# Attention and MLP kernel on one core: where the input and the probabilities are transposed

## The chip, the cores and the metric

The kernel runs on one core of one Trainium2 chip. Its time is the device time of one execution, in microseconds. The kernel before took 1684.08 us, the median of 3 runs (1683.23 to 1684.34).

## The reference

The input x has 4 batches of 2048 rows of 512 float32 numbers. The first half is a causal attention with one head of 512:

```
x_norm = (x - mean) / sqrt(var + eps) * gamma + beta
q, k, v = x_norm @ wq, x_norm @ wk, x_norm @ wv
probs = softmax(causal(q @ k.T / sqrt(512)))
x1 = layernorm(x + (probs @ v @ wo + x))
```

The second half is an MLP of three 512x512 products with SiLU behind the first two, a softmax router over 8 experts of which the two best give gates, a scatter-add of gated rows into the first 8 rows, and a last layernorm.

## The kernel before

**Numbers.** Each large product is done as three fp32r products of split operands (`split_product`, L334 to L336): hi x hi, lo x hi and hi x lo. So each operand needs its hi part, which ScalarE or VectorE rounds, and its lo part, which VectorE gets as the difference (f32 value less hi).

**Opening.** The weights are folded into m = wq wk' and wvo = wv wo (`fold_weights`, TensorE), so that scores are (x_norm m) x_norm' and v is x_norm wvo.

**Stages.** A batch has 16 tiles of 128 query rows, in 4 groups of 4. Tile t has `chunks(t)` = t//4 + 1 chunks of keys, up to 512 keys each. Every engine has its own queue in a written order, in functions named `tile(b, t)`; the engines meet at semaphores. The loop over batches starts at tile 2 and has tiles 0 and 1 of the next batch at its end, so its back edge lies between tiles 1 and 2. On TensorE tile t is:

- scores of tile t+1, chunk after chunk, into one PSUM bank per chunk (12 matmuls for 512 keys), with the transposes of tile t's chunk 0 ahead of the last chunk;
- for each chunk of tile t: transposes of the next chunk's probabilities (`turn_probs`, L1221), then `attend`, the chunk's product with v (3 matmuls per 128 keys);
- in tiles 2, 6 and 10 the projections of the next group: `project_v` of its first tile, `project_g`, three more `project_v`. For the next batch's first group they lie in tile 15.

**Probabilities.** ScalarE's `exp` writes a row tile `probs` in SBUF. TensorE turns it in 128x128 blocks into one of two PSUM banks, ScalarE rounds it to `pt_hi` (L628), VectorE takes the difference to `pt_lo` (L859). Both have two buffers, so chunk n waits for `attend` of chunk n-2 (`pv_done`).

**Input.** x is loaded in pairs of tiles into `xin`, normalised in place (statistics on VectorE, L823; the reciprocal root on GpSimd; scale and shift on ScalarE, L580), turned by TensorE into PSUM (`turn_x`, L1159), given gamma and beta by ScalarE (L564), and split by VectorE (`split_x`, L841 and L843) into `xt_hi` and `xt_lo`. This is done in units of half a pair in the tiles ahead of the projections.

**VectorE's order in tile t** is: residual of tile t-1, maxima of tile t+1's chunks but the last, difference of chunk 0, last maximum and bias (`row_bias`), row sum, difference of chunk 1, the pieces for x, `norm_behind` (statistics of the outputs), and then the differences of chunks 2 and 3.

**SyncE's queue** issues, in order, each tile's load of x for the residual, and the stores of x1 and of the output of earlier tiles. In the last tile it also loads x1 for the second half, with `load_x1` (L345): rows of 32 elements, 128 bytes, laid out so that VectorE's transpose of 32x32 blocks (L994) gives the full transpose.

## Time and profile before

| | us |
|---|---|
| median of 3 runs | 1684.08 |
| profiled execution | 1682.32 |
| its span, first to last instruction | 1680.3 |
| TensorE busy | 1650.4 |
| VectorE busy | 828.1 |
| ScalarE busy | 671.6 |
| GpSimd busy | 282.6 |

Busy time of TensorE counts overlapping matmuls once. A row of the timeline gives the start, the duration, the engine and the line; x4 at its end means four in a row that were merged, and a bracket gives the idle time ahead and what ended it. The second number of a group is the mean duration of one. DMA moved 92.58 MB, at 55 GB/s over the span.

### The profile page before, as it was taken

What the parts mean: (1) busy time and instruction counts of PE and PEld (TensorE: products, weight loads), DVE (VectorE), ACT (ScalarE), POOL (GpSimd) and SP (SyncE); (2) the same over time, 40 slices, a digit from 0 to 9 for tenths busy, and PEclk for the clock granted to TensorE, in tenths of its full rate; (3) what the DMA queues carried; (4) which work ended last, traced back from release to release, by engine and by line L of the source; (5) the groups of instructions that cost most, each with busy time, mean ns of one, the idle gap of its engine ahead of it and who ended that gap; (6) DMA issues with size and microseconds to landing.
All of it is one profiled execution on the core that took longest, in us unless ns stands there. A gap on an engine that the chain in (4) does not pass through costs nothing.

```text
span 1680.3 us, 23574 instructions
## 1 busy us (share of the span) xinstructions
PE 1650.4 (98%) x7923; PEld 1369.7 (82%) x7923; DVE 828.1 (49%) x2168; ACT 671.6 (40%) x1301; POOL 282.6 (17%) x491
## 2 busy tenths in 40 slices
PE   7999999999999999999999999999999999999998
PEld 5888888878888888788888888888878888888886
DVE  5454434454453445455343456443456556555563
ACT  5443333443342334343322445332344444444443
POOL 1120201111120111121110112010122212212121
PEclk9999999999999999999999999999999999999999
DMA  4111201121111011121101132111154223132200
GB/s 157 57 51 51 70 32 38 64 71 63 70 51 51 32 50 64 58 101 49 53 19 38 45 100 95 38 57 45 63 115 74 36 39 50 25 50 43 32 0 7
DMA packets 173764, 92.58 MB, mean 55 GB/s; under 512 B 137296, under 2 KB 137296, under 8 KB 173664
## 3 DMA queue, kind: packets, MB, share of 16 engines
q1 hardware_dynamic: 162768, 72.41, 15.8%
q10 hardware_dynamic: 10896, 18.90, 3.6%
q8 instruction: 56, 0.92, 0.2%
q14 instruction: 44, 0.36, 0.1%
HBM read 57.71 MB, written 33.57 MB: 54 GB/s over the span
## 4 chain that ended last, share of the span: by engine, by line
PE 79%; issue 13%; POOL 3%; ACT 3%; DVE 2%; DMA 1%; SPq 0%; ACTq 0%; POOLq 0%; DVEq 0%
PE psum L334 24%; PE psum L336 24%; PE psum L335 24%; PE psum L1221 3%; PE psum L1159 1%; POOL rstd L454 1%; PE psum L1326 1%; PE psum L1325 1%; PE psum L1318 1%; PE psum L1317 1%; ACT xin L580 1%; ACT tok L580 1%; POOL expo L529 1%; ACT affine L564 0%; DVE stats L823 0%
## 5 line engine op out<-in xcount | busy, mean ns | idle before, releaser
L334 PE MATMUL psum<-xt_hi,g_hi 128*128 128x512 f32 (+3 forms) x640 | 239.5, 374 | 0.4 <-DVE g_lo L849 0.4
L628 ACT ACTIVATE pt_hi<-psum 128x512 fp32r<-128x512 f32 (+3 forms) x160 | 84.8, 530 | 369.6 <-PE psum L1221 363.7
L336 PE MATMUL psum<-xt_lo,g_hi 128*128 128x512 f32 (+3 forms) x640 | 230.0, 359 | 0.0
L335 PE MATMUL psum<-xt_hi,g_lo 128*128 128x512 f32 (+3 forms) x640 | 229.2, 358 | 0.0
L334 PE MATMUL psum<-v_hi,pt_hi 128*128 128x512 f32 x544 | 222.8, 410 | 1.8 <-DVE pt_lo L859 1.4
L336 PE MATMUL psum<-v_lo,pt_hi 128*128 128x512 f32 x544 | 213.1, 392 | 0.0
L335 PE MATMUL psum<-v_hi,pt_lo 128*128 128x512 f32 x544 | 212.8, 391 | 0.0
L451 POOL TENSOR_TENSOR var_eps<-meanvar,eps 128x2 f32<-128x2 f32 (+1 forms) x97 | 19.3, 199 | 1048.8 <-DVE meanvar L827 1046.7
L864 DVE TENSOR_REDUCE rowmax<-psum 128x1 f32<-128x512 f32 (+3 forms) x160 | 97.5, 610 | 197.7 <-PE psum L336 197.2
L746 ACT ACTIVATE act_f<-psum 128x512 f32<-128x512 f32 x128 | 76.5, 598 | 210.0 <-PE psum L336 210.0
L529 POOL TENSOR_TENSOR expo<-euler,shifted 128x32 f32<-128x32 f32 x16 | 86.9, 5430 | 298.0 <-DVE shifted L1061 298.0
L334 PEld LDWEIGHTS psum<-xt_hi,g_hi 128*128 128x128 f32 x640 | 121.2, 189 | 15.5 <-DVE g_lo L849 0.5
L859 DVE TENSOR_TENSOR pt_lo<-psum,pt_hi 128x512 fp32r<-128x512 f32 (+3 forms) x160 | 97.4, 609 | 73.4 <-ACT pt_hi L628 71.7
L336 PEld LDWEIGHTS psum<-xt_lo,g_hi 128*128 128x128 f32 x640 | 120.3, 188 | 16.1
L335 PEld LDWEIGHTS psum<-xt_hi,g_lo 128*128 128x128 f32 x640 | 120.8, 189 | 15.1
L336 PEld LDWEIGHTS psum<-v_lo,pt_hi 128*128 128x128 f32 x544 | 102.2, 188 | 22.9
L334 PEld LDWEIGHTS psum<-v_hi,pt_hi 128*128 128x128 f32 x544 | 102.3, 188 | 22.2 <-issue 2.9
L335 PEld LDWEIGHTS psum<-v_hi,pt_lo 128*128 128x128 f32 x544 | 102.6, 189 | 17.7
L580 ACT ACTIVATE tok<-tok,shift,rstd 128x512 f32<-128x512 f32 x128 | 97.3, 809 | 46.5 <-POOL shift L456 46.4
L849 DVE TENSOR_TENSOR g_lo<-psum,g_hi 128x512 fp32r<-128x512 f32 x64 | 44.2, 691 | 130.9 <-ACT g_hi L577 130.9
L612 ACT ACTIVATE probs<-psum,bias 128x512 f32<-128x512 f32 (+3 forms) x157 | 97.6, 628 | 25.1 <-PE psum L1221 11.9
L853 DVE TENSOR_TENSOR v_lo<-psum,v_hi 128x512 fp32r<-128x512 f32 x64 | 44.0, 688 | 121.4 <-ACT v_hi L602 121.4
(145 smaller groups left out, 3401.7 us busy)
## 6 DMA issues: line engine op xcount, KB each, us to landing
xin<-in_x ACTq DMA_DIRECT2D x64, 256.0 KB, 2.8
tok<-in_x SPq DMA_DIRECT2D x64, 256.0 KB, 2.6
x_scratch<-tok SPq DMA_DIRECT2D x64, 256.0 KB, 2.0
out_dram<-tok SPq DMA_DIRECT2D x64, 256.0 KB, 2.0
x_in<-x_scratch SPq DMA_DIRECT2D x64, 256.0 KB, 4.2
xin<-in_w_t ACTq DMA_DIRECT2D x8, 256.0 KB, 2.8
w_sb<-in_w_t SPq DMA_DIRECT2D x1, 1024.0 KB, 5.2
raw<-in_wq_t SPq DMA_DIRECT2D x1, 768.0 KB, 6.1
```

The source lines that it names most:

```text
L334: pe.matmul(o, ws, ms, start=first, stop=False, skip_group_check=True)
L335: pe.matmul(o, w_lo, ms, start=False, stop=False, skip_group_check=True)
L336: return pe.matmul(o, ws, m_lo_, start=False, stop=last, skip_group_check=True)
L529: pool.tensor_tensor(expo[:], euler[:], shifted[:], ALU.pow).then_inc(exp_ready, 1)
L580: return act.activation(o, y, ACT.Identity, bias=shift[:, slot:slot + 1], scale=rstd[:, slot:slot + 1])
L612: act.activation(probs[:, at:at + w], psum[:, c, 0:w], ACT.Exp, bias=bias[:, t % 2:t % 2 + 1], scale=SCALE, accum_out=sums4[:, t % 2, c:c ...
L628: act.activation(pt_hi[:, n % 2, 0:w], psum[:, turn_bank(turn_use(t, c)), 0:w], ACT.Copy).then_inc(pt_hi_ready, 1)
L746: act.activation(act_f[:, n % 2, :], psum[:, bank, :], ACT.Silu)
L849: dve.tensor_tensor(g_lo[:, j, :], psum[:, j, :], g_hi[:, j, :], ALU.subtract).then_inc(g_ready, 1)
L859: dve.tensor_tensor(pt_lo[:, n % 2, 0:w], psum[:, turn_bank(turn_use(t, c)), 0:w], pt_hi[:, n % 2, 0:w], ALU.subtract).then_inc(pt_ready, 1)
L864: return dve.tensor_reduce((rowmax if chunks(t) == 1 else rowmax4)[:, c:c + 1], psum[:, c, 0:width(t, c)], AX.X, ALU.max)
L1221: last = pe.transpose(psum[:, turn_bank(n), k * P:(k + 1) * P], probs[:, key_start(t, c) + k * P:key_start(t, c) + (k + 1) * P], ident[:])
```

## The change

Three things are changed.

- The normalised pairs of x are stored to DRAM (`xn_scratch`), loaded back as 128-byte rows into `xt_b` (the memory of `xt_lo`) and turned by VectorE into `xt_a` (the memory of `xt_hi`), a group of four tiles at a time; ScalarE applies gamma and beta back into `xt_b`, and VectorE splits from there, in four units of 128 x 512. The first group of the first batch is still turned by TensorE.
- The probabilities of tiles 8 to 15 (`FAR`) take the same way: SyncE stores each chunk to `p_scratch`, loads it back into `probs` as 128-byte rows, and VectorE turns it into `pt_f` (the memory of `pt_lo`).
- In the opening TensorE does 14 matmuls of the identity, the fold is ordered anew, and three pairs of x are loaded early into a free part of `xt_a`.

The diff, cut to its core:

```diff
+    FAR = 2 * GROUP
+    P_BLOCK = P * GROUP * P
+    p_scratch = nc.dram_tensor("p_scratch", [2 * GROUP * P_BLOCK], F32, kind="Internal").ap()
     x1_scratch = nc.dram_tensor("x1_scratch", [B * S, D], F32, kind="Internal").ap()
+    xn_scratch = nc.dram_tensor("xn_scratch", [B * S, D], F32, kind="Internal").ap()
...
+        unrounded = ExitStack()
+        xt_a = sb("xt_a", [P, DC, S], F32, unrounded)
+        xt_b = sb("xt_b", [P, DC, S], F32, unrounded)
+        unrounded.close()
         xt_hi = sb("xt_hi", [P, DC, S], F32R, stage01)
         xt_lo = sb("xt_lo", [P, DC, S], F32R, stage01)
-        affine = sb("affine", [P, 512], F32, stage01)
...
+        turned = ExitStack()
+        pt_f = sb("pt_f", [P, 2, GROUP * P], F32, turned)
+        turned.close()
         pt_lo = sb("pt_lo", [P, 2, GROUP * P], F32R, stage01)
...
+        def x_pair(n, first):
+
+            if first and n in EARLY:
+                return xt_a[:, n - 1, 2 * GROUP * P:4 * GROUP * P].rearrange("p (s d) -> p s d", s=2)
+            return xin[:]
...
+        def columns(g):
+            return slice(GROUP * g * P, GROUP * (g + 1) * P)
+
+        def through_dram(b, t, c):
+
+            tiles_with = [u for u in range(FAR, TILES) if chunks(u) > c]
+            return b * len(tiles_with) + tiles_with.index(t) + 1
+
+        def p_rows(t, c):
+
+            at = (t % 2 * GROUP + c) * P_BLOCK
+            return p_scratch[at:at + P * width(t, c)]
...
+                if pair == 1:
+                    for n in EARLY:
+                        sp.dma_start(x_pair(n, True), pair_rows(x, 0, n)).then_inc(x_early_loaded[n - EARLY[0]], DMA)
...
+            def store_p(b, t, c):
+                w, at = width(t, c), key_start(t, c)
+                sp.wait_ge(probs_ready, 1 + b * CHUNKS + BEFORE[t] + c + 1)
+                sp.dma_start(p_rows(t, c).rearrange("(r n) -> r n", n=w), probs[:, at:at + w]).then_inc(p_stored[c], DMA)
+
+            def load_p(b, t, c):
+
+                w, at = width(t, c), key_start(t, c)
+                sp.wait_ge(p_stored[c], through_dram(b, t, c) * DMA)
+                rows_of = p_rows(t, c).rearrange("(r j k q i) -> q j k r i", j=LANES, k=w // P, q=QUADRANTS, i=LANES)
+                for q in range(QUADRANTS):
+                    sp.dma_start(probs[q * LANES:(q + 1) * LANES, at:at + w].rearrange("j (k r i) -> j k r i", k=w // P, i=LANES),
+                                 rows_of[q]).then_inc(p_loaded[c], DMA)
...
+            def store_xn(b, pair, first=False):
+                sp.wait_ge(x_normed, b * PAIRS + pair + 1)
+                sp.dma_start(pair_rows(xn_scratch, b, pair), x_pair(pair, first)).then_inc(xn_stored, DMA)
+
+            def load_x(b, pair):
+                sp.dma_start(xin[:], pair_rows(x, b, pair)).then_inc(x_loaded, DMA)
+
+            def load_xq(b, g):
+
+                rows_of = xn_scratch[bass.ds(b * S + g * (GROUP * P), GROUP * P), :].rearrange("(t j) (c q i) -> q j c t i", j=LANES, q=QUADRANTS, i=LANES)
+                for c in range(DC):
+                    for q in range(QUADRANTS):
+                        sp.dma_start(xt_b[q * LANES:(q + 1) * LANES, c, columns(g)].rearrange("j (t i) -> j t i", i=LANES),
+                                     rows_of[q][:, c]).then_inc(xq_loaded[g % 2], DMA)
...
+                g, k = t // GROUP, t % GROUP
                 slot = t % SLOTS
                 sp.wait_ge(out_stored[slot], 1 + (b * USES + t // SLOTS) * DMA)
                 sp.dma_start(tok[:, slot, :], x[bass.ds(b * S + t * P, P), :]).then_inc(res_loaded[slot], DMA)
+                if t == TILES - 1 and not last:
+                    sp.wait_ge(scores_ready, b * CHUNKS + BEFORE[t] + 1)
+                    load_xq(b + 1, 0)
+                normed = None
...
+                if normed:
+                    store_xn(*normed)
+                if t >= FAR:
+                    for c in range(chunks(t)):
+                        store_p(b, t, c)
+                    for c in range(2):
+                        load_p(b, t, c)
...
+                if t >= FAR:
+                    for c in range(2, chunks(t)):
+                        load_p(b, t, c)
+                if normed:
+                    sp.wait_ge(xn_stored, stored(*normed))
+                    to_load = ahead(b, first_half(g) if k else second_half(g), last)
+                    if to_load:
+                        load_x(*to_load)
+                if k == GROUP - 1:
+                    if g + 2 < GROUPS:
+                        sp.wait_ge(scores_ready, b * CHUNKS + 1)
+                        load_xq(b, g + 2)
+                    elif g + 2 > GROUPS and not last:
+                        sp.wait_ge(scores_ready, b * CHUNKS + BEFORE[t] + 2)
+                        load_xq(b + 1, g + 2 - GROUPS)
...
+            for t in range(2):
                 tile(0, t, before=False)
+            for n in EARLY[0:2]:
+                store_xn(0, n, first=True)
+            sp.wait_ge(xn_stored, stored(0, EARLY[1]))
+            load_xq(0, 1)
+            store_xn(0, EARLY[2], first=True)
+            tile(0, 2, before=False)
...
+            def affine_x(b, g, c):
+
+                act.wait_ge(xq_turned, (b * GROUPS + g - 1) * DC + c + 1)
+                act.activation(xt_b[:, c, columns(g)], xt_a[:, c, columns(g)],
+                               ACT.Identity, bias=beta_sb[:, c:c + 1], scale=gamma_sb[:, c:c + 1]).then_inc(affine_ready, 1)
...
+                if t == 1 and not before:
+                    norm_x(b, EARLY[2], first=True)
+                if k == 2 and ahead(b, second_half(g), last):
+                    norm_x(*ahead(b, second_half(g), last))
                 if more and k == 2:
-                    turn_x(b, g + 1, 2)
-                if t == TILES - 2 and not last:
-                    turn_x(b + 1, 0, 0)
+                    affine_x(b, g + 1, 2)
+                    affine_x(b, g + 1, 3)
                 if t == TILES - 1 and not last:
-                    turn_x(b + 1, 0, 2)
-                if more and k == 1:
-                    norm_x(b, 2 * (g + 1) + 1)
+                    affine_x(b + 1, 0, 2)
+                    affine_x(b + 1, 0, 3)
...
+                if k == GROUP - 1 and ahead(b, first_half(g), last):
+                    norm_x(*ahead(b, first_half(g), last))
                 if t and not (t == TILES - 1 and not last):
                     norm_behind(b, t - 1, (0, 1) if before or t > 1 else (0,))
+                if more and k == 1:
+                    affine_x(b, g + 1, 0)
+                    affine_x(b, g + 1, 1)
                 if t == TILES - 2 and not last:
-                    norm_x(b + 1, 1)
+                    affine_x(b + 1, 0, 0)
+                    affine_x(b + 1, 0, 1)
...
+                    else:
+                        act.wait_ge(xn_stored, stored(B - 1, PAIRS - 1))
...
+            def norm_x(b, pair, first=False):
+                if first and pair in EARLY:
+                    dve.wait_ge(x_early_loaded[pair - EARLY[0]], DMA)
+                else:
+                    dve.wait_ge(x_loaded, (pair + 1) * DMA if first else (b * PAIRS + pair - 2) * DMA)
+                if not first or pair:
+                    dve.wait_ge(x_normed, b * PAIRS + pair)
+                y = x_pair(pair, first)
+                statistics(lambda s: y[:, s - 2, :], 2, 4, x_variance)
+
+            def split_first_x(u):
+                at = slice(2 * (u // 2) * P, 2 * (u // 2 + 1) * P)
+                c = slice(2 * (u % 2), 2 * (u % 2) + 2)
+                dve.wait_ge(affine_ready, 1 + u + 1)
+                dve.tensor_copy(xt_hi[:, c, at], xt_b[:, c, at]).then_inc(xt_hi_ready, 1)
+                dve.wait_ge(xt_hi_ready, u + 1)
+                dve.tensor_tensor(xt_lo[:, c, at], xt_b[:, c, at], xt_hi[:, c, at], ALU.subtract).then_inc(xt_ready, 1)
+
+            def turn_x(b, g, c):
+                dve.wait_ge(xq_loaded[g % 2], (2 * b + (g + 1) // 2) * DC * LOADS)
+                dve.transpose(xt_a[:, c, columns(g)], xt_b[:, c, columns(g)]).then_inc(xq_turned, 1)
+
+            def split_x(b, g, c):
+                n = (b * GROUPS + g) * XUNITS + c + 1
                 dve.wait_ge(affine_ready, 1 + n)
-                dve.tensor_copy(xt_hi[:, c:c + 2, at:at + 256], value).then_inc(xt_hi_ready, 1)
+                dve.tensor_copy(xt_hi[:, c, columns(g)], xt_b[:, c, columns(g)]).then_inc(xt_hi_ready, 1)
                 dve.wait_ge(xt_hi_ready, n)
-                dve.tensor_tensor(xt_lo[:, c:c + 2, at:at + 256], value, xt_hi[:, c:c + 2, at:at + 256],
+                dve.tensor_tensor(xt_lo[:, c, columns(g)], xt_b[:, c, columns(g)], xt_hi[:, c, columns(g)],
                                   ALU.subtract).then_inc(xt_ready, 1)
...
+            def turn_probs(b, t, c):
+
+                n, w, at = BEFORE[t] + c, width(t, c), key_start(t, c)
+                dve.wait_ge(p_loaded[c], through_dram(b, t, c) * LOADS)
+                dve.wait_ge(pv_done, 1 + b * CHUNKS + n - 1)
+                dve.transpose(pt_f[:, n % 2, 0:w], probs[:, at:at + w]).then_inc(probs_turned, 1)
 
             def chunk_max(b, t, c):
                 dve.wait_ge(scores_ready, b * CHUNKS + BEFORE[t] + c + 1)
@@ -903,37 +1047,37 @@
                 more = g + 1 < GROUPS
                 if t:
                     residual(b, t - 1)
-                if t + 1 < TILES:
-                    for c in range(chunks(t + 1) - 1):
-                        chunk_max(b, t + 1, c)
+                early_maxima = range(chunks(t + 1) - 1) if t + 1 < TILES else range(0)
+                for c in early_maxima[0:1]:
+                    chunk_max(b, t + 1, c)
+                if t >= FAR:
+                    turn_probs(b, t, 0)
+                for c in early_maxima[1:]:
+                    chunk_max(b, t + 1, c)
                 split_probs(b, t, 0)
-                if more and k == 0:
-                    split_x(b, g + 1, 0)
+                if t >= FAR:
+                    turn_probs(b, t, 1)
                 if t + 1 < TILES:
                     row_bias(b, t + 1)
                 row_sum(b, t)
                 if chunks(t) > 1:
                     split_probs(b, t, 1)
-                if more and k == 0:
+                if more and k == 1:
+                    for c in range(DC):
+                        turn_x(b, g + 1, c)
+                if more and k == 2:
+                    split_x(b, g + 1, 0)
                     split_x(b, g + 1, 1)
-                if more and k == 2:
-                    split_x(b, g + 1, 2)
-                if t == TILES - 2 and not last:
-                    split_x(b + 1, 0, 0)
                 if t == TILES - 1 and not last:
                     split_x(b + 1, 0, 2)
-                if k == 3 and g + 2 < GROUPS:
-                    norm_x(b, 2 * (g + 2))
-                if k == 3 and g + 2 == GROUPS and not last:
-                    norm_x(b + 1, 0)
+                if k == GROUP - 1 and ahead(b, first_half(g), last):
+                    norm_x(*ahead(b, first_half(g), last))
                 if t:
                     norm_behind(b, t - 1, z=2 if before or t > 1 else 1)
                 elif before:
                     norm_behind(b - 1, TILES - 1)
                 if t + 1 < GROUP:
...
                 if t == TILES - 1 and not last:
                     split_x(b + 1, 0, 3)
...
                 if chunks(t) > 2:
+                    if t >= FAR:
+                        turn_probs(b, t, 2)
                     split_probs(b, t, 2)
...
                 if chunks(t) > 3:
+                    if t >= FAR:
+                        turn_probs(b, t, 3)
                     split_probs(b, t, 3)
                 if t == TILES - 1 and last:
                     split_wr()
+                if t == TILES - 2 and not last:
+                    for c in range(DC):
+                        turn_x(b + 1, 0, c)
+                    split_x(b + 1, 0, 0)
+                    split_x(b + 1, 0, 1)
                 if more and k == 2:
+                    split_x(b, g + 1, 2)
                     split_x(b, g + 1, 3)
                     split_v(b, GROUP * (g + 1))
...
+                if t == 0 and not before:
+                    norm_x(b, EARLY[2], first=True)
+                if k == 1 and ahead(b, second_half(g), last):
+                    norm_x(*ahead(b, second_half(g), last))
...
-                    pe.wait_ge(xt_ready, 1 + b * (GROUPS * XUNITS) + g * XUNITS + 3 + half)
+                    pe.wait_ge(xt_ready, 1 + b * (GROUPS * XUNITS) + g * XUNITS + (3 + half if first else 2 + 2 * half))
...
+                if tile % GROUP == 0 and tile:
+                    pe.wait_ge(xt_ready, 1 + (b * GROUPS + tile // GROUP + 1) * XUNITS)
...
             def turn_probs(b, t, c):
+                if t >= FAR:
+                    return
...
                 turn_probs(b, t, 0)
-                if more and k == 0:
-                    turn_x(b, g + 1, 0)
                 if t + 1 < TILES:
                     score(b, t + 1, chunks(t + 1) - 1)
...
+            for _ in range(WARMING):
+                pe.matmul(psum[:, XBANK, 0:P], ident[:], ident[:], start=True, stop=True)
+            fold_weights(0, 0, (0, 1))
+            turn_x(0)
+            fold_weights(0, 0, (2, 3))
+            turn_x(1)
+            for c in range(1, DC):
+                fold_weights(0, c, range(DC))
+            for c in range(2):
+                fold_weights(1, c, range(DC - 1))
+            turn_x(2)
+            for c in range(2, DC):
+                fold_weights(1, c, range(DC - 1))
+            turn_x(3)
+            for c in range(DC):
+                fold_weights(1, c, (DC - 1,))
```

## Rows read from the trace of the kernel before

**Rows 1.** The page, part 1: busy time, share of the span, instructions.
```profile
PE 1650.4 (98%) x7923; PEld 1369.7 (82%) x7923; DVE 828.1 (49%) x2168; ACT 671.6 (40%) x1301; POOL 282.6 (17%) x491
```
**Rows 2.** What TensorE waited for: us in total, times, longest.
```profile
PE psum L1159 <- ACT xin L580: 11.9, 5, 9.4
PE psum L1221 <- issue: 4.7, 2, 2.4
PE psum L1159 <- ACT affine L564: 2.1, 4, 0.5
```
**Rows 3.** TensorE's groups by form, the transposes: busy us, mean ns, idle before.
```profile
L1221 PE MATMUL psum<-ident,probs 128*128 128x128 f32 x544 | 85.4, 272 | 4.8 <-issue 4.7
L1159 PE MATMUL psum<-ident,xin 128*128 128x128 f32 x256 | 39.6, 278 | 14.0 <-ACT xin L580 11.9 <-ACT affine L564 2.1
```
**Rows 4.** Timeline of TensorE in tile 12 of batch 1: start, duration.
```profile
573.92 0.60 PE L1221 MATMUL psum<-ident,probs 128*128 128x128 f32 x4
574.28 0.48 PE L334 MATMUL psum<-v_hi,pt_hi 128*128 128x512 f32 x1
574.60 0.39 PE L335 MATMUL psum<-v_hi,pt_lo 128*128 128x512 f32 x1
574.83 0.39 PE L336 MATMUL psum<-v_lo,pt_hi 128*128 128x512 f32 x1
```
**Rows 5.** Timeline of VectorE in the same tile.
```profile
574.12 0.42 DVE L864 TENSOR_REDUCE rowmax<-psum 128x1 f32<-128x256 f32 x1 [0.23 <-PE psum L336]
...
575.26 0.69 DVE L859 TENSOR_TENSOR pt_lo<-psum,pt_hi 128x512 fp32r<-128x512 f32 x1
575.87 1.28 DVE L823 BATCH_NORM_STATS2 stats<-tok 128x6 f32<-128x512 f32 x2
...
577.28 0.15 DVE L827 BATCH_NORM_AGGREGATE meanvar<-stats 128x2 f32<-128x6 f32 x1
```
**Rows 6.** VectorE's and ScalarE's groups by form.
```profile
L994 DVE STREAM_TRANSPOSE x1t_f<-x_in 128x512 f32<-128x512 f32 x64 | 41.6, 688 | 2.7 <-DMA x_in<-x_scratch 2.7
L859 DVE TENSOR_TENSOR pt_lo<-psum,pt_hi 128x256 fp32r<-128x256 f32 x28 | 11.9, 424 | 25.3 <-ACT pt_hi L628 25.0
...
L628 ACT ACTIVATE pt_hi<-psum 128x512 fp32r<-128x512 f32 x100 | 59.5, 596 | 324.1 <-PE psum L1221 321.1 <-issue 3.0
L628 ACT ACTIVATE pt_hi<-psum 128x256 fp32r<-128x256 f32 x28 | 10.6, 378 | 16.5 <-PE psum L1221 16.5
```
**Rows 7.** Timeline of VectorE in tile 2 of batch 1.
```profile
375.48 0.43 DVE L841 CAST xt_hi<-affine 128x512 fp32r<-128x512 f32 x1
375.94 0.69 DVE L843 TENSOR_TENSOR xt_lo<-affine,xt_hi 128x512 fp32r<-128x512 f32 x1
```
**Rows 8.** Timeline of TensorE in tile 2 of batch 1.
```profile
370.32 0.54 PE L1221 MATMUL psum<-ident,probs 128*128 128x128 f32 x3 [2.39 <-issue]
...
373.61 0.60 PE L1159 MATMUL psum<-ident,xin 128*128 128x128 f32 x4
...
379.36 0.39 PE L334 MATMUL psum<-wvo_hi,xt_hi 128*128 128x512 f32 x1
```
**Rows 9.** Timeline of TensorE from tile 14 to tile 15 of batch 0.
```profile
325.57 0.60 PE L1221 MATMUL psum<-ident,probs 128*128 128x128 f32 x4
...
327.76 0.47 PE L334 MATMUL psum<-v_hi,pt_hi 128*128 128x512 f32 x1
```
**Rows 10.** Timeline of TensorE in the opening.
```profile
10.10 0.78 PE L334 MATMUL psum<-raw_hi 128*128 128x512 f32 x1
10.68 0.63 PE L335 MATMUL psum<-raw_hi,raw_lo 128*128 128x512 f32 x1
...
37.89 0.39 PE L334 MATMUL psum<-xt_hi,m_hi 128*128 128x512 f32 x1
```
**Rows 11.** Timeline of SyncE's DMA queue in the last tile.
```profile
1232.20 11.44 SPq L345 DMA_DIRECT2D x_in<-x_scratch  x8
```
**Rows 12.** Timeline of VectorE in the last tile.
```profile
1240.79 1.31 DVE L994 STREAM_TRANSPOSE x1t_f<-x_in 128x512 f32<-128x512 f32 x2 [2.69 <-DMA x_in<-x_scratch]
```
**Rows 13.** Two windows: engines' busy time, granted clock, DMA share, GB/s.
```profile
1238.00:1240.00 2.00, 2.00 (x13) 1.65 (x12) 0.10 (x2) 0.60 (x1) 1.66 (x6) 1.00 1.00 158
10.00:15.00 5.00, 5.00 (x15) 3.98 (x14) 3.52 (x6) 2.58 (x5) 0.00 (x0) 1.00 1.06 403
```

More of the change, by code:

```diff
@@ L213, in attention_mlp @@
                 TURNS += [("v", t + 1 + j) for j in range(GROUP)]
-            TURNS += [("p", t, c) for c in range(chunks(t))]
+            if t < FAR:
+                TURNS += [("p", t, c) for c in range(chunks(t))]
         def turn_use(t, c):
@@ L497, in batch @@
                         tile(b + 1, t)
-            for pair in range(FIRST_PAIRS):
+            for pair in range(FIRST_PAIRS - 1):
                 norm_x(0, pair)
@@ L662, in tile @@
                         turn_probs(b, t, c)
-                    if more and k == 2 and c == chunks(t) - 1:
-                        turn_x(b, g + 1, 3, more=not (last and g + 2 == GROUPS))
                     if c < n_next:
@@ L934, in tile @@
                     split_v(b, t + 1)
-                if t == TILES - 2 and not last:
-                    split_x(b + 1, 0, 1)
                 if t == TILES - 1 and not last:
@@ L959, in tile @@
                         split_v(b, GROUP * (g + 1) + j)
-                if more and k == 0:
-                    norm_x(b, 2 * (g + 1) + 1)
-                if t == TILES - 2 and not last:
-                    norm_x(b + 1, 1)
+                if t == 0 and not before:
+                    norm_x(b, EARLY[2], first=True)
+                if k == 1 and ahead(b, second_half(g), last):
+                    norm_x(*ahead(b, second_half(g), last))
                 from_tile = TILES - 1 - GROUP
```

198 lines of the change are left out of this document (84 added, 114 removed).

## The prediction

> **What bounds the kernel now.** I read the page's busy shares first [rows 1]: TensorE is busy 98% of 1680.3 us, VectorE 49%, ScalarE 40%. So TensorE's queue is the kernel, and whatever leaves it is worth its issue time. Then what TensorE waited for [rows 2]: 11.9 us for the normalised input, of which 9.37 us is the opening, 4.7 us at the loop's back edges, 2.1 us for the affine step. There is next to no idle time to win; only instructions can be taken away, and every wait that is added counts in full. Third, the transposes by form [rows 3]: 544 of probabilities and 256 of x, with a duration of 272 to 278 ns.
>
> That duration is not the price, because matmuls overlap. The price is read from starts [rows 4]: four transposes start at 573.92, the next product at 574.28, so 0.36 us; and the first product behind them takes 0.32 us to the next start where its successors take 0.23. Together 0.45 us for four, 0.113 us each.
>
> **Removed from TensorE.** Probabilities of tiles 8 to 15: 9+10+...+16 = 100 blocks in each of 4 batches, 400. Of x: 256 less the 16 of the first group, 240. 640 x 0.113 = 72.5 us. With them go about 3 us of waits for x and affine behind the opening [rows 2]. ScalarE's copy and VectorE's difference stay, only from another source.
>
> The Trainium skill (TensorE: Matmul & The Clock Gate, Part 4: PE-mode transpose) gives about 275 ns for one transpose in a kernel, and the trace agrees as a duration. By it the 640 would be worth 176 us and the kernel would come to about 1506; the starts of rows 4 show the pace, so I don't use it.
>
> **Moved to VectorE.** 100 x 4 blocks of probabilities and 240 of x, in units like the 128x512 transpose that stage 2 has, 0.688 us, a new one about every 0.61 [rows 6]. It is half idle, so the sum of 100 us is no concern; its order is. The p transposes of chunks 0 and 1 stand ahead of the last score and are covered. That of chunk 2 can't be early: its buffer is shared with chunk 0, and VectorE reaches it only after the statistics. In the old order TensorE had turned the chunk already, so that behind the statistics only a difference was left.
>
> Let S be TensorE's start of the first thing behind the last score. In tile 12 [rows 4, 5] S is 573.92; the maximum starts at S+0.20, the difference of chunk 1 at S+1.34, the statistics at S+1.95, and they end at S+3.51 (577.28+0.15). A wider next chunk adds 0.1 to 0.2 us (0.42 us for 256 elements [rows 6], 0.69 for 512). From there the new chain of chunk 2 is transpose, round, difference: 0.69+0.60+0.69 and 0.2 for handovers, 2.2 us at 512 wide (1.4 at 256: 0.42+0.38+0.42 [rows 6]; 1.8 at 384). TensorE wants chunk 2 after two products of 12 matmuls, 2 x 2.72 = 5.44 behind S. One batch, tile by tile:
> - 8: about 0. 12: about 0. 13 and 14: S+5.7 and S+5.8, together 0.7 us.
> - 9: four transposes of x stand ahead of the statistics, +2.44: S+7.4, 2.0 us.
> - 10: two split units of x stand there, each 1.07 us (0.46 from 375.48 to 375.94, 0.61 for the difference) [rows 7], +2.14: S+7.6, 2.2 us. The second two end some 0.1 us late for the projection.
> - 11: the input's statistics stand there, 1.5 us, as before, but with the transpose behind them: S+7.1, 1.6 us (last batch 0.2).
> - 6: no chunk 2, but the projection of tile 8's v now waits for all four units of x: S + 2.0 + 4 x 1.07 + 1.5 = 7.8, with handover 8.0, wanted at 5.25: 2.8 us.
> - 2: the same, in a shorter tile. S was 373.61, the projection began at 379.36 with two transpose groups before it, so it is wanted at S+4.9 [rows 8]. VectorE had its maximum and sum at S+1.8 [rows 7], half a microsecond later now since tile 1 gained transposes; 2.3 + 4.28 + 1.5 + 0.6 + 0.2 = 8.9: 4.0 us.
> - 15: in tile 14 four transposes and two split units of the next batch stand behind the last difference. It ends near S+7.3; 2.4 for the transposes and 2.3 for the splits bring the residual to S+12.1; residual 0.7, transpose, round and difference 2.2: the first product at S+15.0, where tile 14's last one ended at S+10.7. 4.3 us; before, the gap was 2.19 [rows 9], of which 12 transposes were 1.36 and 0.83 idle. So 3.5 us, three times.
>
> Per batch 0.7+2.0+2.3+1.6+2.8+4.0 = 13.4 us; four batches less 1.4 for the last tile 11 are 52.2, tile 15 adds 10.5.
>
> **Last tile of all.** x1 for stage 2 is loaded by the same SP queue, now behind 1 MB of probability loads. Eight such 256 KB issues took 11.44 us [rows 11], so 1 MB holds SP for 5.7 us. The last exp is at about S+7.5; store, 5.7 us of loads, the other stores between them 1, then 5.7 us of x1 and its landing 2.9 (1240.79 less 1237.92 [rows 11, 12]): about S+24. VectorE waits for it in order, ahead of chunk 2's transpose; 1.3 for two transposes and 2.2 for the chain give S+28, where TensorE could have been there at S+20: 8 us. With 1.5 us at its first product that is 9.5.
>
> **DMA itself.** Otherwise the round trip is covered: exp of the last chunk is some 3 us before the tile's end, and VectorE asks for the first loaded chunk 3.5 us into the next tile, the second 3 us later. 26 MB of p and 16 MB of x come back in short rows. In stage 2 such a load kept the queues at a share of 1.00 at 158 GB/s [rows 13], so a 1 MB tile costs 7 us of a tile of some 22. The cost of the covered part is 0; if each came 2 us late in 32 tiles, +64; below 0 it can't be, for nothing in it replaces TensorE work. I take 0, its nearest rows being 7 of 22.
>
> Here the Trainium skill speaks against the change: DMA: Bandwidth & Descriptors (Specifications) wants at least 512 bytes a transfer for line rate, and these rows are 128 bytes. The trace agrees: 158 GB/s against 403 with the weights' long rows at 10 to 15 us [rows 13].
>
> **Opening.** TensorE starts at 9.37 on x, now on the weights at about 7.7, after 14 warming matmuls; its first products went at a pace of 0.43 (10.10 to 10.68 and on), half the later one, at a granted clock shown as 1.00 [rows 10, 13]. About 5 us of slow pace hold 2.3 us of loss. The fold's last quarter is put last, which covers x's second pair. The fold ended at 37.89 [rows 10]; 96 products need 21.8 us, the chain of weights lets the second half go from 22.3, and I get 32 to 34: -5 us (bounds 0 and -8). Two early pairs normalised on ScalarE, 3 us, lie beside the projection of g.
>
> **Sum.** 1682.3 (the profiled execution, 1.8 under the median of 1684.1): -72.5 -3 -5 +52.2 +10.5 +9.5 = 1674.0; on the median's footing 1675.8. I say 1676.
>
> **Rivals.**
> A. The DRAM trip is late (slower). Mechanism: SP's queue is in order; it stands at exp of the last chunk and only then sends loads of a tile, and VectorE's in-order queue stops at the first missing chunk with the maxima behind it. For: 1.43 us per 256 KB of issue. Against: some 2 us of slack at chunk 0 and 1.5 behind it. It decides once a load is over 3 us later than I have it; at 2 us in 24 four- or three-chunk tiles, +48: 1722.
> B. The waits are half hidden. VectorE's blocks would have to end sooner than their rows; against it is that each is a sum of measured durations. 72 halved: 1640.
> C. The clock falls in the new gaps (slower). The loop's gap of 2.39 us was followed by a first product at ordinary pace [rows 8], but seven new gaps are about 4 us and one is 8. If each is followed by the opening's slow stretch, 2.3 us: 8 x 2.3 = +18: 1694. The Trainium skill (TensorE: Matmul & The Clock Gate, Why this matters for your kernels) warns of idle gaps between bursts; no row here has one in mid-kernel longer than 2.39.
> D. The change moves the work without freeing time: waits of all kinds sum to the removed 72 to 80: within 3 us of 1684.
>
> **Chances.** Forecast 0.50, A 0.10, B 0.17, C 0.15, D 0.08. 0.2% is 3.4 us, about what a measurement of this kernel can tell from none. The forecast's own range is 1664 to 1690 (28 waits, each good to 0.4 us), of which seven in ten lie below 1680.7 and one in ten above 1687.5. Faster 0.35+0.17+0.02 = 0.54, same 0.16, slower 0.30. Range 1640 to 1704: B's centre, and a part of A.
>
> **What would show it.** L1221's transposes fall to 144 and x's to 16, and the sum of TensorE's work falls by 72 us. In a tile-10 stretch the first product of chunk 2 waits about 2 us for pt_lo. The projection behind tiles 2 and 6 waits 4 and 3 us for xt_lo. TensorE's idle time is about 30 - 8 + 72 = 94 us. In the last tile VectorE waits for x1 near 8 us. If VectorE waits for DMA in most tiles, A; if products pace at 0.43 behind the gaps, C. Wrong altogether if idle time is under 50 or over 130 us.

## The result and the profile after

The changed kernel takes 1771.18 us (median of 4 runs, 1763.91 to 1772.61) where the one before took 1683.78 beside it: 1.0506 times as long, 95% interval 1.0492 to 1.052. I had said 1676, with a range of 1640 to 1704. The sign was wrong.

The page, part 1, answers to [rows 1]; the span grew from 1680.3 to 1768.6 us:

```profile
PE 1629.9 (92%) x7311; PEld 1330.3 (75%) x7311; DVE 929.5 (53%) x2340; ACT 664.8 (38%) x1241; POOL 290.2 (16%) x491
```

7923 - 640 + 28 is 7311: the transposes are gone and 14 warming matmuls (two instructions each) have come. But TensorE's busy time fell by 20.5 us and not by 67, its idle time (span less busy) rose from 29.9 to 138.7, and the mean granted clock fell from 1.000 to 0.970. Two things are to be explained: 109 us more idle, and work that ran slower. What TensorE waited for (us in all, times, longest), which answers to [rows 2], the transposes that are left (busy, mean ns), to [rows 3], and what VectorE waited for in DMA:

```profile
PE psum L354 <- DVE pt_lo L996: 78.4, 35, 9.3
PE psum L354 <- DVE xt_lo L979: 40.0, 15, 6.1
PE psum L1379 <- issue: 5.4, 2, 3.0
...
L1379 PE MATMUL psum<-ident,probs 128*128 128x128 f32 x144 | 24.0, 276 | 5.4 <-issue 5.4
...
DVE pt_f L1004 <- DMA probs<-p_scratch: 46.2, 31, 5.2
DVE stats L945 <- DMA xin<-in_x: 28.0, 5, 8.3
DVE xt_a L972 <- DMA xt_b<-xn_scratch: 9.3, 3, 3.6
```

The first three rows say who hands over last, not who is late: VectorE is half idle, and stands 46 us itself for probabilities that come back from DRAM. So each wait has to be followed one step further. TensorE's timeline at the five kinds of long waits, the bracket giving the wait:

```profile
342.50 0.80 PE L354 MATMUL psum<-v_hi,pt_hi 128*128 128x512 f32 x1 [8.01 <-DVE pt_lo L996]
343.10 0.63 PE L355 MATMUL psum<-v_hi,pt_lo 128*128 128x512 f32 x1
343.52 0.63 PE L356 MATMUL psum<-v_lo,pt_hi 128*128 128x512 f32 x1
...
401.29 0.79 PE L354 MATMUL psum<-wvo_hi,xt_hi 128*128 128x512 f32 x1 [6.08 <-DVE xt_lo L979]
...
512.78 0.76 PE L354 MATMUL psum<-v_hi,pt_hi 128*128 128x512 f32 x1 [3.55 <-DVE pt_lo L996]
...
554.18 0.50 PE L354 MATMUL psum<-v_hi,pt_hi 128*128 128x512 f32 x1 [1.93 <-DVE pt_lo L996]
...
1328.77 0.80 PE L354 MATMUL psum<-v_hi,pt_hi 128*128 128x512 f32 x1 [9.28 <-DVE pt_lo L996]
```

They are tile 15 (batch 0), tile 2, tile 8, tile 10 and the last tile. For tile 8 my list had "about 0"; in batches 0 to 2 it is 3.9, 3.6 and 3.6 us. The chain of waits through it, in order of time (start, duration, what):

```profile
501.19 1.53 ACT xin L705 x2
...
502.74 0.42 SPq L457
...
503.27 2.84 DMA p_scratch<-probs
...
506.13 0.66 SPq L444
...
508.18 2.33 DMA probs<-p_scratch
...
510.53 0.72 DVE pt_f L1004
...
511.28 0.64 ACT pt_hi L755
...
511.94 0.70 DVE pt_lo L996
...
512.78 0.76 PE psum L354
```

and ScalarE's exp of the first chunk of that tile:

```profile
497.30 0.69 ACT L738 ACTIVATE probs<-psum,bias 128x512 f32<-128x512 f32 x1
```

The probabilities lay ready at 498.0. SyncE sent them only at 503.27, because its queue held the store of the normalised x first (L457), which waited for ScalarE until 502.7. From the store to the first loaded chunk it is 7.2 us (2.84, three issues before the fourth, 2.33 to land). Without the 5.3 us lost in the queue the chunk would have landed near 505.3, when VectorE came to ask for it (its last maximum ended at 505.69). The chunk had no slack to lose. The last batch has no next x to store, so there nothing stands ahead of tile 8's probabilities. The exp of its first chunk ended at 1153.36, and SyncE sent them at once:

```profile
1153.48 1.39 SPq L436 DMA_DIRECT2D p_scratch<-probs  x3
```

TensorE's first product of that tile waited for nothing (0.2 us between its start and the one before).

How SyncE's queue looks from tile 14 to tile 15:

```profile
323.34 8.73 SPq L467 DMA_DIRECT2D xt_b<-xn_scratch  x16
332.25 0.42 SPq L457 DMA_DIRECT2D xn_scratch<-xin  x1
332.78 2.35 SPq L436 DMA_DIRECT2D p_scratch<-probs  x4
335.92 5.39 SPq L444 DMA_DIRECT2D probs<-p_scratch  x8
```

Eight 64 KB loads hold it for 5.4 us, 0.67 us each, so a tile with four chunks costs it 10.7 us of load issues where I had 5.7. The size hardly counts here: four loads of 32 KB, in tile 8 of the last batch, took 2.55 us, 0.64 each. The sixteen loads of x come on top.

A third place is in tile 15, where SyncE gives out the next pair of x (L460) only at 348.16, behind all loads of probabilities. VectorE stood for it in batches 0 to 2 (6.1, 7.2 and 8.3 us, most of the 28.0 above), with the last split of x behind:

```profile
352.80 1.29 DVE L945 BATCH_NORM_STATS2 stats<-xin 128x6 f32<-128x512 f32 x2 [6.05 <-DMA xin<-in_x]
```

That split's end is what TensorE waited for inside `project_g` (0.9, 2.3 and 3.2 us).

The slower work is seen in windows of 1 us (us, busy time of each engine, then the granted clock, DMA share and GB/s), here around the wait at tile 15:

```profile
337.00:338.00 1.00, 0.00 (x0) 0.00 (x0) 0.97 (x3) 0.00 (x0) 0.00 (x0) 0.69 0.54 112
338.00:339.00 1.00, 0.00 (x0) 0.00 (x0) 1.00 (x2) 0.00 (x0) 0.00 (x0) 0.50 0.54 86
...
346.00:347.00 1.00, 1.00 (x4) 0.72 (x3) 0.71 (x2) 0.27 (x1) 0.00 (x0) 0.50 0.64 102
347.00:348.00 1.00, 1.00 (x5) 0.82 (x4) 0.00 (x0) 0.00 (x0) 0.00 (x0) 0.69 0.65 101
348.00:349.00 1.00, 1.00 (x6) 0.82 (x5) 0.00 (x0) 0.00 (x0) 0.00 (x0) 1.00 0.57 90
```

TensorE stopped at 334.5. The clock fell to 0.50, which is 1.2 instead of 2.4 GHz, 3 us later, and stayed there for about 5 us after work had begun again at 342.50; starts are 0.43 us apart in it (343.10, 343.52) and not 0.23. The same happens behind the waits of tile 2 in every batch, of tile 8 in the three that have one, and behind some of about 2 us.

### The profile page after: what moved, and what is told of

Its sections match the earlier page's. It is cut to its first block, busy times and chain, and to the rows that moved or that the text cites. A ratio compares the mean times of both kernels' runs of the same rounds, so it can differ in the third digit from the quotient of the medians.

```text
span 1768.6 us, 23775 instructions
## 1 busy us (share of the span) xinstructions
PE 1629.9 (92%) x7311; PEld 1330.3 (75%) x7311; DVE 929.5 (53%) x2340; ACT 664.8 (38%) x1241; POOL 290.2 (16%) x491
## 4 chain that ended last, share of the span: by engine, by line
PE 51%; issue 21%; SPq 9%; DVE 8%; DMA 5%; POOL 3%; ACT 3%; POOLq 0%; DVEq 0%; ACTq 0%
PE psum L354 16%; PE psum L356 16%; PE psum L355 16%; SPq L444 6%; DMA p_scratch<-probs 2%; DVE stats L945 2%; DMA xin<-in_x 1%; POOL rstd L583 1%; SPq L467 1%; DVE xt_a L972 1%; DMA probs<-p_scratch 1%; ACT xin L705 1%; PE psum L1475 1%; PE psum L1476 1%; PE psum L1468 1%
## 5 line engine op out<-in xcount | busy, mean ns | idle before, releaser
L354 PE MATMUL psum<-v_hi,pt_hi 128*128 128x512 f32 x544 | 226.2, 416 | 79.3 <-DVE pt_lo L996 78.4
L356 PE MATMUL psum<-v_lo,pt_hi 128*128 128x512 f32 x544 | 219.1, 403 | 0.0
L355 PE MATMUL psum<-v_hi,pt_lo 128*128 128x512 f32 x544 | 219.1, 403 | 0.0
L755 ACT ACTIVATE pt_hi<-pt_f 128x512 fp32r<-128x512 f32 (+2 forms) x112 | 65.7, 587 | 386.7 <-DVE pt_f L1004 377.4
L354 PEld LDWEIGHTS psum<-v_hi,pt_hi 128*128 128x128 f32 x544 | 106.3, 195 | 119.0 <-DVE pt_lo L996 71.9
L354 PE MATMUL psum<-wvo_hi,xt_hi 128*128 128x512 f32 x256 | 106.1, 414 | 33.6 <-DVE xt_lo L979 33.6
L356 PEld LDWEIGHTS psum<-v_lo,pt_hi 128*128 128x128 f32 x544 | 106.0, 195 | 23.9
L355 PEld LDWEIGHTS psum<-v_hi,pt_lo 128*128 128x128 f32 x544 | 106.4, 196 | 20.3
L354 PE MATMUL psum<-xt_hi,m_hi 128*128 128x512 f32 x256 | 101.2, 395 | 6.4 <-DVE xt_lo L979 6.4
```

The costliest lines, as they stand in the source:

```text
L354: pe.matmul(o, ws, ms, start=first, stop=False, skip_group_check=True)
L355: pe.matmul(o, w_lo, ms, start=False, stop=False, skip_group_check=True)
L356: return pe.matmul(o, ws, m_lo_, start=False, stop=last, skip_group_check=True)
L755: act.activation(pt_hi[:, n % 2, 0:w], turned_, ACT.Copy).then_inc(pt_hi_ready, 1)
```

## The experiments

Theory Q: SyncE's one in-order queue makes the two ways through DRAM disturb each other. Theory V: the order of VectorE's queue is the price, as the prediction had it. Theory C: the clock's fall is a large part. Each run's ratio is to the kernel before, measured beside it on the same chip, and runs are compared by these ratios; the changed kernel stands at 1.0506.

**The parts alone.** Three kernels; the first sets `FAR = TILES`, the second adds only `p_scratch`, `store_p`, `load_p` and VectorE's `turn_probs` to the kernel before, the third only the opening.

```diff
-    FAR = 2 * GROUP
+    FAR = TILES
```

> The changed kernel with the probabilities of all sixteen tiles turned by TensorE again; the input's way through DRAM and the opening stay. It saves 240 transposes (27 us) and 3 us of opening. If only VectorE's order costs (the waits of the prediction for tiles 2 and 6, 8 us a batch, less at tile 15), it gives 1684 - 27 - 3 + 36 = 1690. If the clock falls in each wait as well, some 16 us more: 1706. If the slow part is the way of the probabilities alone, it comes in at 1655.

> The kernel before with only the probabilities of tiles 8 to 15 sent through DRAM; input and opening as before. It saves 400 transposes (45 us). If the long waits at tiles 8 and 15 come from SyncE's queue, which then holds no store and no strided loads of x, they are gone, and only the last tile (13 us) and small waits (8 us) are left: about 1660, the best of these kernels. If instead the way of the probabilities is late in itself, tile 8 and tile 15 keep about 4 and 4 us a batch, with the clock's loss 45 us in all: about 1690.

> The kernel before with only the opening reordered: fourteen warming matmuls and the fold in the new order, nothing through DRAM. First group's projection starts 3 us earlier: 1680.5. If the early start is taken back by the first waits of batch 0: 1684.

Measured: input alone, with the opening, 1714.53 us (1.0176, 1.0159 to 1.0193); probabilities alone 1690.57 (1.0041, 1.0029 to 1.0054); opening alone 1679.43 (0.997, 0.9957 to 0.9982). So the opening gives 5 us (3 to 7), as forecast. Both ways through DRAM are a loss, each although it takes 27 or 45 us of work from TensorE. And alone they add 1.76% and 0.41%, together 5.06%: 2.9%, or 49 us (give or take 4), arises only when both are in. VectorE's order alone doesn't reach that: the waits in my list that need both parts, those of tiles 9, 10 and 15, come to 28 us at most. I was wrong, too, that the probabilities alone would give 1660.

**The clock.** Small matmuls nobody reads, ahead of the waits:

```diff
+            def fill(n):
+                for _ in range(n):
+                    pe.matmul(psum[:, XBANK, 0:P], ident[:], ident[:], start=True, stop=True)
...
                 n = BEFORE[t] + c
+                fill(FILL_A.get((t, c), 0))
```

> The changed kernel with small matmuls whose result nobody reads put into TensorE's queue just ahead of the waits: 32 ahead of the product for v of tile 4, 16 ahead of that of tile 8, 26 at tile 8, 12, 14 and 10 at tiles 9 to 11, 58 at tile 15, each 0.115 us and in sum shorter than the wait they stand in. They make nothing come sooner, so if waits alone cost the time stays at 1771 (no more than 5 us off). If the clock falls in the idle time and what follows then runs at half pace, idle time is as before counting the fillers but the granted clock goes from 0.97 to about 0.99 and the time falls by some 30 us, to about 1741.

Measured 1771.32 (1.0516, 1.0498 to 1.0534). The time did not move, but my price was wrong: each is two instructions and took 0.227 us, so the fillers were longer than the waits. It is still the most useful trace of the study, since the clock stays up until the last 12 us of it (0.999). Its page and the fillers' group:

```profile
PE 1737.5 (98%) x8655; PEld 1458.3 (82%) x8655; DVE 928.0 (52%) x2340; ACT 663.5 (37%) x1241; POOL 290.4 (16%) x491
...
L1339 PE MATMUL psum<-ident 128*128 128x128 f32 x1344 | 154.6, 275 | 0.0
```

1737.5 - 154.6 = 1582.9 us of real work at full clock. The kernel before had 1650.4; less 72.5 for the transposes and plus 5.3 for the warming makes 1583.2. So the forecast's 0.113 us a transpose was right, and the changed kernel's 1629.9 hold 47 us of slower work. Taken over the stretches at the lower clock, half of TensorE's busy time in them is 38 us; the other 9, as an estimate, are the ends and starts of matmuls at some 40 more stops. The Trainium skill (TensorE: Matmul & The Clock Gate, Part 4: PE-mode transpose) gives 275 ns; by that the work would have come down by 176 us, which this trace excludes.

Then half as many:

> As the kernel with the small matmuls, which took 0.227 us each and not 0.115, so that 58 of them lasted 13.1 us where the wait was 8.4. Here half as many: 16 before v of tile 4, 8 before v of tile 8, 13 at tile 8, 6, 7 and 5 at tiles 9 to 11, 29 at tile 15, 70 us in the whole run, all inside the waits. They make no data come sooner. Theory of the clock: the granted clock comes to 0.99 or more, the half-pace stretches behind the waits go, and the time falls by 35 to 45 us, to about 1730. Rival, that only the waits cost and the clock's fall lies inside them: 1771, no change.

Measured 1761.85 (1.0465, 1.0448 to 1.0483), clock 0.989:

```profile
PE 1683.6 (96%) x7983; PEld 1393.5 (79%) x7983; DVE 928.3 (53%) x2340; ACT 663.4 (38%) x1241; POOL 290.3 (17%) x491
...
L1339 PE MATMUL psum<-ident 128*128 128x128 f32 x672 | 79.8, 275 | 0.0
```

Real work is now 1683.6 - 79.8 = 1603.8, 26 us less than 1629.9. Fillers and idle together are 1759.6 - 1603.8 = 155.8 where 138.7 was idle: 17 us more. Of 26 us that the clock gave back, 9 (7 by the ratios, give or take 4) reached the end. That is somewhat too little, because at the end of the last batch fillers stood where the changed kernel hardly waits (tile 11) or waits less long (tile 15: 6.6 us of fillers, 3.8 of wait). At tile 10 of that batch, ahead of both, the kernel was 12.0 us ahead; of this one and of the changed kernel:

```profile
1192.45 0.50 PE L354 MATMUL psum<-v_hi,pt_hi 128*128 128x512 f32 x1 [0.36 <-DVE pt_lo L996]
...
1204.48 0.50 PE L354 MATMUL psum<-v_hi,pt_hi 128*128 128x512 f32 x1 [1.93 <-DVE pt_lo L996]
```

So about half of what the clock gave back can count. For the rest TensorE came sooner to its next wait and stood longer: before tile 8 of batches 0 to 2 it waited 2.8 to 2.9 us on top of 3.0 of fillers, where the wait was 3.6 to 3.9. Theory C holds for the mechanism and fails for the size: half or more of the slow pace is paid inside a chain that TensorE does not set.

**SyncE's queue.** First the store of x behind the probabilities at tiles 8 and 12, then the first group of x in 4 DMAs in place of 16 (the same bytes in long rows, so that those columns hold other values than the reference's). The edit of the first:

```diff
-                if normed:
+                late = t >= FAR and k == 0
+                if normed and not late:
                     store_xn(*normed)
...
+                if normed and late:
+                    store_xn(*normed)
```

> The changed kernel with one thing moved in SyncE's queue: at tiles 8 and 12 the store of the normalised x, which waits for ScalarE, comes behind the stores and the first loads of the probabilities. Theory of the queue: TensorE's wait at tile 8 (3.7 us, and about 1.8 us of slow work behind it) goes in all four batches, about 20 us: 1750. The rival, that the way through DRAM is late at tile 8 in itself: the wait shrinks by less than 1 us, 1768. The waits of tiles 2, 6, 9 to 11 and 15 stay in both.

> The changed kernel in which the first group of x of batches 1 to 3 is loaded by 4 DMAs instead of 16 (the same bytes in long pieces, so that those columns hold other values than the reference's). SyncE spends about 2.5 us instead of 8.7 there. Theory of the queue: VectorE's wait for that load (2.8 us) and the probabilities' delay (1.25 us) go, and TensorE's wait at tile 15 falls from 8.4 to 4.3 us, which VectorE's own work gives: about 13 us in three batches, 1758. If VectorE's work alone sets the wait: 1771.

Measured 1750.01 (1.0388, 1.0371 to 1.0406) and 1760.39 (1.0453, 1.0436 to 1.047). The first moves one line and gives 20 us (21 in microseconds), as expected, though from three batches and not four; TensorE's wait at tile 8 is gone. VectorE's wait for probabilities from DRAM, in that kernel:

```profile
DVE pt_f L1007 <- DMA probs<-p_scratch: 15.3, 16, 2.1
```

In the changed kernel it was 46.2 us in 31 waits. The second gives 9 (11 in microseconds): TensorE's wait at tile 15 falls from 8.01 to

```profile
341.10 0.80 PE L354 MATMUL psum<-v_hi,pt_hi 128*128 128x512 f32 x1 [5.84 <-DVE pt_lo L1002]
```

It changes two things at once, the number of DMAs and the length of their rows. And it does not free the whole 5.9 us that SyncE's issues of x became shorter, for the first store of probabilities, sent 4.2 us earlier, while the loads of x and the store behind them were under way, took 5.6 us to land and not 3.1. The chains of this kernel and of the changed one:

```profile
328.61 5.60 DMA p_scratch<-probs
...
332.78 3.13 DMA p_scratch<-probs
```

So near tile 15 what the transfers do to each other seems to count beside the queue; no run separates the two.

**VectorE's order.** The third chunk ahead of x and LayerNorm work, with and without a shift of x's split; and the latter's better form where only x goes through DRAM:

```diff
+                if t >= FAR:
+                    turn_probs(b, t, 2)
+                    split_probs(b, t, 2)
```

> The changed kernel with VectorE's and ScalarE's order changed: the third chunk of probabilities of tiles 8 to 15 is turned and split right behind the second and ahead of the work on x and the LayerNorm, and the split of the next x begins a tile earlier. If VectorE's order makes the waits, those at tiles 9, 10 and 11 (5.1 us a batch) go, that at tile 2 falls from 6.0 to about 1.2 us and that at tile 6 from 2.4 to 0; with the slow stretches behind them 12 to 17 us a batch: 1710 to 1725. If those waits are for DRAM and not for VectorE, they stay: 1765.

> The changed kernel with the order of the third chunk alone changed (the split of x stays where it was; in the run that moved both, VectorE then stood 3.8 us for ScalarE at the end of tiles 1, 5 and 9). VectorE's order: the waits at tiles 9, 10 and 11 go (5.1 us a batch, some 7 with the slow work behind them), 1771 - 25 = 1746. If TensorE then only waits at the next tile for what SyncE has not yet loaded, which that failed run would fit as well: 1765 to 1771.

> The kernel before with only the probabilities through DRAM, and the third chunk turned and split right behind the second, ahead of VectorE's work on x and the LayerNorm (in tiles 14 and 15 behind one part of x). In the kernel with the probabilities alone TensorE waited 1.6 to 1.9 us for that chunk at three tiles of every batch, and 1.9 to 2.1 more in tile 15. If VectorE's order makes these waits they go, 20 to 28 us with what is slow behind them: 1665. If the loads or ScalarE make them: 1690 as without the move.

> Only the input through DRAM (and the opening), with the four parts of x scaled a tile earlier and split together: TensorE's wait at tile 2 falls from 6.0 to about 2.7 us and that at tile 6 from 2.4 to 0, with what is slow behind them 25 us in all: 1714 - 25 = 1689. If, as with the third chunk, the wait only moves to TensorE's next stop: 1710.

Measured: 1772.55 (1.0531, 1.0513 to 1.0549); 1776.95 (1.056, 1.0543 to 1.0576); 1687.62 (1.002, 1.0011 to 1.003, where it was 1.0041 without the move); 1712.23 (1.0169, 1.0152 to 1.0186, where it was 1.0176). Four orders, and the most that any gained is 3.5 us. The waits that I named did go; others took their place. TensorE's waits with the third chunk first:

```profile
PE psum L354 <- DVE pt_lo L996: 70.7, 25, 10.9
PE psum L354 <- DVE xt_lo L979: 47.0, 14, 6.1
```

78.4 fell by 7.7 and 40.0 rose by 7.0: x was now late at tile 10 and the residual at tile 15. With only x through DRAM, the shifted split:

```profile
PE psum L354 <- DVE pt_lo L993: 31.5, 21, 3.3
PE psum L354 <- DVE xt_lo L976: 12.3, 5, 3.2
```

where the unshifted one had

```profile
PE psum L354 <- DVE xt_lo L979: 34.5, 12, 6.1
PE psum L354 <- DVE pt_lo L996: 13.6, 15, 1.9
```

The sum went from 48.1 to 43.8. Theory V as "a bad order" falls: the orders tried only chose which wait. VectorE is not full in these tiles either. In the run with the third chunk first it was busy 14.7 of the 19 us before tile 10's projection (212 to 231), and in the rest its queue stood in order for TensorE and ScalarE. In the run that shifted x as well, I had also made VectorE stand 3.8 us for ScalarE at the end of tiles 1, 5 and 9.

**The mends together.** All three orders, and the first load of x1 issued by ScalarE's queue, with VectorE's work on x1 behind its chunks of probabilities; the same for the probabilities alone; and the first with 4 DMAs for the first group of x.

```diff
+                    load_x1(act, 0, 0)
                     act.dma_start(wr_raw[:], wr_t.rearrange("(c p) n -> p c n", p=P)).then_inc(wr_loaded, DMA)
```

> The changed kernel with all the mends at once: the store of x behind the loads of the probabilities at tiles 8 and 12, the third chunk first, the four parts of x scaled at the end of the tile before and split together, and the first load of x1 given out by ScalarE's queue. If these orders are the whole price, 1771 - 21 - 25 - 10 - 10 = 1705, still above before, with the waits of tiles 2 and 15 left. If what is taken off one wait comes back in the next, since SyncE's queue in the last tiles and VectorE in tiles 1 and 2 are near full: 1735.

> The kernel before with the new opening, the probabilities alone through DRAM in VectorE's better order, and the first load of x1 given out by ScalarE's queue so that VectorE does not stand for it ahead of the third chunk. If the orders were all that spoiled this part: 1684 - 5 - 45 + 8 (small waits) + 10 (last tile, clock) = 1652 to 1665, faster than before. If DRAM's way is late in itself: 1680.

> All the mends together, and the first group of x of batches 1 to 3 loaded by 4 DMAs of long pieces instead of 16 (those columns then hold other values than the reference's). With all mends TensorE still waits 10 us at tile 15 of batches 0 to 2, while VectorE stands 3.8 us for this load. If SyncE's sixteen issues are the larger part: the wait falls to 5 or 6 us and the time by about 15 us, to 1702. If the probabilities' own way (store, wait, load, turn, round) sets that wait: below 2 us of gain, 1716.

Measured: 1717.6 (1.0197, 1.0181 to 1.0213); 1678.0 (0.9966, 0.9954 to 0.9978); 1708.95 (1.0142, 1.0118 to 1.0166). All mends take 52 us off the changed kernel. The parts alone, mended, stand at +1.69% (input with the opening) and -0.04% (probabilities, against the opening alone), together 1.65%, where both in one kernel stand at 1.97%. So of the 49 us that arose only from having both, some 5 are left, give or take 5. Which of the mends took how much of the rest, beyond the 20 of SyncE's order alone, was not tried one by one. At tile 15 the wait is 9.89 us with all mends, and with fewer issues

```profile
329.65 0.79 PE L354 MATMUL psum<-v_hi,pt_hi 128*128 128x512 f32 x1 [6.61 <-DVE pt_lo L1004]
```

so the loads of x, their number and short rows together, are a quarter to a third of that wait (10.08 to 7.79 and 9.70 to 6.26 in the next two batches); the 9 us gained lie between my two numbers.

The kernel with the probabilities alone, mended, is as fast as the one with the opening alone (0.9966 against 0.997). Both beat the kernel before by 5 to 6 us and the changed one by 90. TensorE's waits in it:

```profile
PE psum L345 <- DVE pt_lo L905: 26.2, 15, 8.9
PE psum L1224 <- ACT xin L622: 6.8, 3, 2.3
PE psum L1288 <- issue: 5.1, 2, 2.6
```

Its TensorE is busy 1621.6 us of a span of 1676.2, the opening alone has 1655.2 of 1678.9. It does 45 us less of transposes; busy time is 34 less (11 lost to half pace), idle time 31 more.

## Why the prediction was wrong

The terms of its sum, against the trace:

| step | said | measured |
|---|---|---|
| 640 transposes | -72.5 | -72.5 (1582.9 of work against 1583.2 worked out) |
| opening | -5 | -5.0 alone (3 to 7); the first projection at 34.54, not 32 to 34, against 37.89 [rows 10] |
| tile 2 | 4.0 a batch | 5.9, 6.1, 3.8, 6.0 |
| tile 6 | 2.8 | 2.4 to 2.5 |
| tiles 9, 10, 11 | 2.0, 2.3, 1.6 | 1.6 to 2.1, 1.9 and 0.5, 1.5 |
| tile 15 | 4.3 | 8.0 to 8.8, and 0.9 to 3.2 more inside `project_g` |
| last tile | 8 and 1.5 | 9.3 and 3.8 |
| tile 8 | 0 | 3.6 to 3.9 in batches 0 to 2, 0 in the last |
| TensorE idle | 94 | 138.7 |
| slower work | 0 | 47, of which 38 at the lower clock |

Work, slower work and idle time, 1583.2 + 47 + 138.7, make the span of 1768.6; the 47 is itself a difference, so what this confirms is the 1583.2 alone.

1. The step that failed first is "DMA itself": "The cost of the covered part is 0". It looked at bandwidth (7 us of 22) and not at the queue. At tile 8 the trip was just covered, with no slack for anything ahead of it in the queue. SyncE's in-order queue costs 20 us there (tile 12's line moved with it), shown by moving one line. The loads of x ahead of tile 15 cost 9 more, queue and transfer together. I had written the mechanism down as rival A, 0.10, but put it at the last exp and at "2 us of slack", and never walked SyncE's queue through a tile with `store_xn` and `load_xq` in it. Rival A's 1722 was the nearest of the rivals' numbers (it took 24 tiles of three or four chunks, where there are 32).
2. "Eight such 256 KB issues took 11.44 us [rows 11], so 1 MB holds SP for 5.7 us" carried a price per byte over to smaller DMAs. Most of it is paid per DMA: 32 KB cost 0.64 us, 64 KB 0.67, 256 KB 1.43. Sixteen for a tile's probabilities are 10.7 us, and sixteen more for x.
3. The clock was left out of the sum and given +18 in rival C, as 8 gaps. It is 38 of the 47 us of slower work, behind every wait of 3 us and more. That at most 12 us of 26 came back when it was mended says that it is not the main cause of the time. The Trainium skill (TensorE: Matmul & The Clock Gate, Why this matters for your kernels) had the warning; the trace of before could not show it, as its longest wait in mid-kernel was 2.39 us [rows 8].
4. Each wait was priced by itself and then summed, as if a mended wait stayed mended. The waits of VectorE's order came out near their numbers, but for tile 2, and yet moving them gave next to nothing. With everything mended, the probabilities' part is worth under 4 us (0.9966 against 0.997), though 45 us of transposes are gone: 31 us came back as idle time, some 6.7 in each of the first three batches and 10 in the last tile, and 11 at the lower clock. My reading is that the transposes between TensorE's products were also the time in which the results of VectorE and ScalarE arrived; no run shows that by itself. The nearest to it is rival D, "moves the work without freeing time", for which I had no trace and gave 0.08.

At tile 2 the wait was 2 us longer than said, because VectorE's two pairs of splits began late and the last took long. In batch 1, the residual ahead of the splits, and the last difference:

```profile
391.54 0.75 DVE L1027 SCALAR_TENSOR_TENSOR tok<-psum,rinv,tok 128x512 f32<-128x512 f32 x1 [2.99 <-POOL tok L605]
...
399.68 1.56 DVE L979 TENSOR_TENSOR xt_lo<-xt_b,xt_hi 128x512 fp32r<-128x512 f32 x1
```

VectorE stood 3.0 us for GpSimd, whose two roots and then the doubling of the residual's x (L605) came behind VectorE's four transposes and statistics; so the splits began 4.3 us behind S (389.69, where S is TensorE's start behind the last score) and not 2.3. The last difference took 1.56 us where others take 0.69, while GpSimd's next L605 ran. My sum had no term for GpSimd.

Open is what makes up the rest of tile 15's wait. Loads of x through GpSimd's queue, which would have taken them from SyncE altogether, were not tried.

## What to carry to other kernels

When a change sends data through DRAM, walk the issuing engine's queue instruction by instruction through the tile in which most is in it: what each one waits for, what stands behind it, and its cost per DMA. When work is taken off the busiest engine, ask which latencies it was covering; where its neighbours hand results over within a microsecond or two, the time saved can turn into waits. Try the halves of a change one by one: here each half's loss and the loss from having both told more than any trace.

## What the runs showed that I had not expected

- The cost of issuing: on SyncE 0.67 us for a 64 KB load of probabilities in 128-byte rows (0.55 for one of x, 8.73 for sixteen), 0.64 for 32 KB, 1.43 for 256 KB, while a store of 256 KB took 0.4 to 0.9; the trip of a chunk from store to use took 7.2 us.
- Behind the waits of 3.5 to 9.3 us, the granted clock went to 0.50 between 2.0 and 5.3 us after TensorE had stopped and came back 3.9 to 5.5 us after work resumed, which cost 1.7 to 2.8 us of work each time. With small fp32 matmuls of the identity in the waits it stayed up (0.999).
- Giving back 26 us of slow work gained 9 at the end, 12 at the most.
